# Cross-attention and a mixture of experts: ranks counted in sets of tiles, one-hots beside attention, returns by products of 32 columns, warm-up products

## The reference

```python
def _L0_xattn_ref(q, k, v):
    ...
    qh = q.reshape(b * h, d // h, m)
    kh = k.reshape(b * h, d // h, -1)
    vh = v.reshape(b * h, c // h, -1)
    ...
    qk = jnp.einsum('bdm,bdn->bmn', qh, kh) * scale
    sm = jax.nn.softmax(qk, axis=-1)
    ret = jnp.einsum('bmn,bcn->bcm', sm, vh)
    return ret.reshape(b, c, m)
...
    gate_logits = jnp.einsum('bsd,de->bse', x, gate_kernel)
    top_k_weights, top_k_indices = jax.lax.top_k(gate_logits, TOP_K)
    top_k_weights = jax.nn.softmax(top_k_weights.astype(jnp.float32), axis=-1).astype(x.dtype)
    ...
    out = jnp.einsum('bse,bsem,emd->bsd', combine, inter, wo_kernel)
...
x = x + _L0_xattn_ref(_layernorm(x, axis=-1), ctx_2048, ctx_2048)
x = x + _L0_ffn_ref(_layernorm(x, axis=-1), ...)
```

## Time and profile before

| | us |
|---|---|
| median of 3 runs (lowest, highest) | 517.07 (514.99, 517.77) |
| the profiled execution | 516.18 |
| its span, first to last instruction | 514.4 |
| mean granted TensorE clock | 0.924 of 2.4 GHz |

### The profile page before, as it was taken

One profiled execution on the slowest core, in us unless ns is written; L12 is line 12 of the kernel. 1 busy time (PEld: TensorE's weight loads), 2 busy tenths in 40 slices (PEclk: granted clock), 3 DMA queues, 4 the chain that ended last, 5 costly groups with the idle time before them and its releaser, 6 DMA issues.

```text
span 514.4 us, 10299 instructions
## 1 busy us (share of the span) xinstructions
PE 446.7 (87%) x3238; PEld 236.4 (46%) x3239; DVE 283.1 (55%) x594; ACT 239.4 (47%) x472; POOL 216.0 (42%) x235
## 2 busy tenths in 40 slices
PE   3938998998989999888148999999999999999991
PEld 3412343443444443224124666666666666666650
DVE  7898989888779989357794222222222222222220
ACT  2755988887768889573002222222222222222220
POOL 8574040627180522295411444444444444444422
PEclk9865999998889999799557999999999999999997
DMA  8776578768686824159921222223322232223321
GB/s 245 219 221 174 132 200 222 228 192 257 182 238 165 257 97 130 46 205 393 395 97 36 32 51 41 41 41 51 51 41 41 43 50 50 41 41 44 50 28 22
DMA packets 42331, 65.42 MB, mean 127 GB/s; under 512 B 6361, under 2 KB 32154, under 8 KB 42298
## 3 DMA queue, kind: packets, MB, share of 16 engines
q1 hardware_dynamic: 28570, 38.49, 26.2%
q0 software_dynamic: 11424, 24.39, 20.2%
q10 hardware_dynamic: 2304, 2.10, 1.3%
HBM read 40.18 MB, written 24.45 MB: 126 GB/s over the span
## 4 chain that ended last, share of the span: by engine, by line
PE 68%; DVE 12%; ACT 7%; DMA 3%; POOL 3%; issue 2%; SPq 1%; ACTq 1%; POOLq 0%; DVEq 0%
PE max_ps L1432 26%; PE pv_ps L1323 9%; PE ring_ps L1444 6%; PE pv_ps L1444 6%; DVE mx L910 6%; PE ring_ps L1306 6%; ACT pt L766 5%; PE ring_ps L1405 3%; PE max_ps L1204 3%; PE max_ps L1276 2%; PE ring_ps L1395 2%; PE ring_ps L1225 2%; PE ring_ps L1289 2%; SPq L384 1%; DVE K L1108 1%
## 5 line engine op out<-in xcount | busy, mean ns | idle before, releaser
L910 DVE TENSOR_REDUCE mx<-max_ps 128x4 f32<-128x1024 f32 x128 | 150.1, 1215 | 18.3 <-PE max_ps L1204 18.1
L766 ACT ACTIVATE pt<-ring_ps 128x512 f32<-128x512 f32 x256 | 139.1, 598 | 35.1 <-PE ring_ps L1306 31.7
L1432 PE MATMUL max_ps<-w_sb,pt 128*128 x312 | 142.1, 599 | 0.9 <-ACT pt L831 0.9
L703 POOL DMA_INDIRECT out<-rb,sidx x39 | 62.0, 1591 | 119.9 <-DVE gidx L1143 58.5
L1167 DVE TENSOR_TENSOR pt<-pt,max_ps 128x512 f32<-128x512 f32 x39 | 26.8, 687 | 121.7 <-PE max_ps L1432 62.7
L1432 PEld LDWEIGHTS max_ps<-w_sb,pt 128*128 128x128 f32 x312 | 57.0, 193 | 58.1 <-issue 58.1
L1323 PE MATMUL pv_ps<-pt,w_sb 128*27 128x256 f32 (+2 forms) x1024 | 81.1, 401 | 1.8 <-ACT pvs L776 1.0
L1204 PE MATMUL max_ps<-K,Q 48*128 48x256 bf16 x512 | 53.4, 289 | 11.6 <-DVE mx L910 11.6
L1306 PE MATMUL ring_ps<-Q,K 50*128 50x256 f16 x512 | 53.1, 288 | 11.6 <-ACT pt L766 10.2
L838 ACT ACTIVATE pt<-ring_ps 128x512 f32<-128x512 f32 x39 | 23.3, 597 | 71.9 <-PE ring_ps L1405 71.9
L695 POOL DMA_INDIRECT pt<-xrow,gidx x39 | 38.7, 992 | 30.3 <-DVE gidx L1118 11.1
(11 more groups left out here) (175 smaller groups left out, 437.2 us busy)
## 6 DMA issues: line engine op xcount, KB each, us to landing
w_sb<-in_L_ffn_w_kernel POOLq DMA_DIRECT2D x16, 512.0 KB, 10.1
K<-k_img SPq DMA_DIRECT2D x14, 448.0 KB, 6.1
Q<-q_img SPq DMA_DIRECT2D x14, 448.0 KB, 7.5
k_img<-kpart SPq DMA_DIRECT2D x28, 192.0 KB, 3.8
q_img<-qpart SPq DMA_DIRECT2D x28, 192.0 KB, 3.4
wo_sb<-in_L_ffn_wo_kernel POOLq DMA_DIRECT2D x8, 512.0 KB, 12.6
acc<-pvs SPq DMA_DIRECT2D x6, 512.0 KB, 3.1
q_sb<-in_x SPq DMA_DIRECT2D x16, 128.0 KB, 4.1
```

Of the source, the lines that this page charges most:

```text
L703: g.indirect_dma_start(xacc, bass.IndirectOffsetOnAxis(ap=sidx[sl.par][:, 0:1], axis=0), y_sb[sl.par], None, compute_op=ALU.add).then_inc( ...
L766: a.activation(pt[:, (2 * i + h) % PTN, :, :], bank(key)[:, :, :], ACT.Exp, scale=SCALE).then_inc(ring_read, 1)
L910: v.tensor_reduce(mx[:, t % 2, :, :, p].rearrange("q mt h -> q h mt"), max_ps[n % 2][:, :, :, :], axis=AX.X, op=ALU.max).then_inc(max_read, 1)
L1432: last = nc.tensor.matmul(flat(max_ps[sl.par][:, bank_of]), lhsT=xT[sl.par][:, k * P:(k + 1) * P], rhs=weight(w, e, KC, k), start=(k == 0) ...
```

## The change

- The four returns to token layout are made of four products of 32 columns each, all into `max_ps[0]`, at steps (14,1), (14,4), (15,2) and after the last; each but the first waits for the residual of the one before.
- `turn_rows` of units 5 and 6 and their logits move to (15,1) to (15,4).
- Ranks are counted in three sets of tiles: 0 to 7, 8 to 13, 14 and 15. For each set PE multiplies `cnt` of all its tiles with the triangle and with ones (`rank`; at (15,0), at (15,7) in front of the last `pv`, and behind the last logits). VectorE (`ranks`) sums over tiles and works out the place in the tile at once, since an expert's start is a multiple of 128; `onehots` makes the set's `onehot_s`, now with two operations and two scalars of each partition, so that it carries the token number. `told` for token numbers goes away.
- The last residual stands in front of the last two choices but behind the choice, the count and the ranks of tiles 8 to 13; the one-hots of tiles 8 to 13 stand behind the last normalisation.
- Behind the last rank product: three warm-up products of 512 columns, one and two more behind the table of tokens and the spare rows.
- The sum of `e2` and `spare` (what GpSimd's reciprocal waits for) come behind `onehot_t`; the weights of slots are divided by the token number (`rtok`).

```diff
-    rows_at[T - 1, 3] = ST - 3
-    logits_at[T - 1, 5] = ST - 3
-    rows_at[T - 1, 6] = ST - 2
+    rows_at[T - 1, 1] = ST - 3
+    logits_at[T - 1, 2] = ST - 3
+    rows_at[T - 1, 3] = ST - 2
+    logits_at[T - 1, 4] = ST - 2
+    unperm_at = {(T - 2, 1): 0, (T - 2, 4): 1, (T - 1, 2): 2}
+    rank_sets = (range(T - 8), range(T - 8, T - 2), range(T - 2, T))
+    ranks_at = {(T - 1, 0): 0, (T - 1, 7): 1}
...
+            def ranks(m):
...
+                v.wait_ge(ranks_full, m + 1)
...
+                for j, t in enumerate(tiles):
+                    then(v.tensor_tensor(before_t[:, t + 1] if t + 1 < T else total[:, :], before_t[:, t], of_tile[:, j], ALU.add))
+                v.tensor_tensor(before_t[:, to], before_t[:, to], in_tile, ALU.add).then_inc(ranks_read, 1)
+                v.wait_ge(ranks_read, m + 1)
...
+                then(v.tensor_tensor(prod, A[:, :, to], before_t[:, None, to].broadcast_to([P, TOPK, n, E]), ALU.mult))
+                then(v.tensor_reduce(slot[:, :, to], prod, axis=AX.X, op=ALU.add))
+                then(v.tensor_copy(slot_i[:, 0, :, to], slot[:, :, to]))
+                then(v.tensor_scalar(slot_i[:, 1, :, to], slot_i[:, 0, :, to], P - 1, None, ALU.bitwise_and))
+                then(v.tensor_copy(slot_f[:, 0, :, to], slot_i[:, 1, :, to]))
+                then(v.tensor_tensor(slot[:, :, to], slot[:, :, to], slot_i[:, 1, :, to], ALU.subtract))
+
+            def onehots(m):
+                for k in range(TOPK):
+                    for t in rank_sets[m]:
+                        v.tensor_scalar(onehot_s[:, k, t, :], iota_s[:, :], slot_f[:, 0, k, t:t + 1], token1f[:, t:t + 1],
+                                        ALU.is_equal, ALU.mult).then_inc(told_done, 1)
...
-            choose(ST - 5, range(T - 8))
+            choose(ST - 5, rank_sets[0])
+            count(0)
             norm_last(normed_last[0:2], x2_last[0:2], 0, 1)
-            count(1, range(T - 8))
+            ranks(0)
+            onehots(0)
 
             residual_last(2)
             stats_last(x2_last[2:3], 2)
-            choose(ST - 3, range(T - 8, T - 4))
+            choose(ST - 2, rank_sets[1])
+            count(1)
             norm_last(normed_last[2:3], x2_last[2:3], 2, 2)
-            count(2, range(T - 8, T - 4))
-            choose(ST - 2, unit_tiles[ST - 2])
-            count(3, unit_tiles[ST - 2])
+            ranks(1)
 
             residual_last(3)
             stats_last(x2_last[3:4], 3)
             choose(ST - 1, unit_tiles[ST - 1])
             norm_last(normed_last[3:4], x2_last[3:4], 3, 3)
-            count(4, unit_tiles[ST - 1])
+            onehots(1)
             choose(ST, unit_tiles[ST])
-            count(5, unit_tiles[ST])
...
+            count(2)
+            ranks(2)
...
-                pe.wait_ge(pv_read, T - 4 + i + 1)
-                for which, to in ((1, 1), (0, 0)):
-                    for f, a, b in ((0, 0, 96), (1, 96, P)):
-                        last = nc.tensor.matmul(max_ps[i % 2][a:b, to, 0, :], lhsT=unperm[:, which, a:b], rhs=pvs[:, f, i % 2, :],
...
+                for which in (1, 0):
+                    for q in range(4):
+                        at = slice(32 * q, 32 * q + 32)
+                        last = nc.tensor.matmul(max_ps[0][at, which, 0, :], lhsT=unperm[:, which, at], rhs=pvs[:, q // 3, i % 2, :],
...
+            def rank(m):
...
+                pe.wait_ge(count_done, m + 1)
+                for b, with_ in ((0, tri), (P, ones)):
...
+            def keep_warm(n):
+
+                for _ in range(n):
+                    nc.tensor.matmul(flat(max_ps[1][:, 1]), lhsT=ident[:, :], rhs=flat(xn), start=True, stop=True)
...
+                if (t, p) in ranks_at:
+                    rank(ranks_at[t, p])
             pv(T - 1, 3, 0)
             pv(T - 1, 3, 1)
             unpermute(3)
...
+            rank(2)
+            pe.wait_ge(ranks_read, 2)
+            keep_warm(3)
+
+            pe.wait_ge(told_done, TOPK * T)
+            for k in range(TOPK):
+                pe.wait_ge(rows_picked, k + 1)
...
```

More of the change, by code:

```diff
@@ L77, in xattn_ffn_kernel @@
             slots["logits", logits_at[t, p]] = len(slots)
-    for n in range(ST - 2, UNITS):
-        if n > ST - 2:
-            slots["rows", n] = len(slots)
+    for n in range(ST - 1, UNITS):
+        slots["rows", n] = len(slots)
         slots["logits", n] = len(slots)
@@ L818, in _ @@
             evac_pv(T - 1)
-            for m in range(ST - 2, UNITS):
-                if m > ST - 2:
-                    evac_rows(m)
+            for m in range(ST - 1, UNITS):
+                evac_rows(m)
                 evac_logits(m)
-            a.wait_ge(gap_done, 5)
+            a.wait_ge(gap_done, 4)
             a.activation(e2[:, :], gap[:, :], ACT.Exp).then_inc(e2_done, 1)
@@ L988, in then, with count @@
                 v.wait_ge(chain, links[0])
-            def count(m, tiles):
-                v.wait_ge(top_done, m)
+            def count(m):
+                tiles = rank_sets[m]
                 a, n = tiles[0], len(tiles)
@@ L995, in count @@
                                      iota_e[:, None, None, :].broadcast_to([P, TOPK, n, E]), ALU.is_equal))
[L996 to L1002, removed]
+                v.tensor_tensor(cnt[:, a:a + n], A[:, 0, a:a + n], A[:, 1, a:a + n], ALU.add).then_inc(count_done, 1)
@@ L1037, in _ @@
             then(v.memset(before_t[:, 0], 0.0))
-            for k in range(TOPK):
-                then(v.tensor_copy(pay[:, 0, k, :], token1[:, :]))
+            then(v.tensor_copy(token1f[:, :], token1[:, :]))
             lead_e = E // 2
@@ L1062, in _ @@
             norm_last(normed_last[3:4], x2_last[3:4], 3, 3)
-            count(4, unit_tiles[ST - 1])
+            onehots(1)
             choose(ST, unit_tiles[ST])
-            count(5, unit_tiles[ST])
[L1067 to L1075, removed]
+            count(2)
+            ranks(2)
+            then(v.tensor_scalar(tiles_i[:, 0], total[:, :], float(P - 1), None, ALU.add))
             then(v.tensor_scalar(tiles_i[:, 1], tiles_i[:, 0], P - 1, None, ALU.bitwise_and))
@@ L1084, in _ @@
                 shift *= 2
[L1086 to L1090, removed]
@@ L1091, in _ @@
-            then(v.tensor_scalar(slot_i[:, 1], slot_i[:, 0], P - 1, None, ALU.bitwise_and))
-            then(v.tensor_tensor(slot_f[:, 1], slot[:, :, :], slot_i[:, 1], ALU.subtract))
+            base = ends[end][:, lead_e - 1:lead_e + E - 1]
+            then(v.tensor_tensor(A[:, :, :, :], A[:, :, :, :], base[:, None, None, :].broadcast_to([P, TOPK, T, E]), ALU.mult))
+            then(v.tensor_reduce(slot_f[:, 1], A[:, :, :, :], axis=AX.X, op=ALU.add))
+            then(v.tensor_tensor(slot_f[:, 1], slot_f[:, 1], slot[:, :, :], ALU.add))
@@ new lines, in _ @@
+                if k == 0:
+                    onehots(2)
+            v.wait_ge(e2_done, 1)
+            v.tensor_scalar(norm[:, :], e2[:, :], 1.0, None, ALU.add).then_inc(norm_in, 1)
+            then(v.scalar_tensor_tensor(spare[:, :, :], cnt[:, :, :], 0.0,
+                                        token1[:, :, None].broadcast_to([P, T, E]), op0=ALU.is_equal, op1=ALU.mult))
+            v.tensor_reduce(spare_own[:, :], spare.rearrange("p t e -> p e t"), axis=AX.X, op=ALU.max).then_inc(spare_done, 1)
@@ L1144, in next_gather @@
                                 ALU.add).then_inc(gidx_done, 1)
-            v.wait_ge(slots_done, 1)
+            then(v.tensor_scalar(rtok[:, :], tok[:, :], 1.0, None, ALU.max))
+            then(v.reciprocal(rtok[:, :], rtok[:, :]))
             then(v.tensor_tensor(spare_of[:, :], spare_of[:, :], spare_own[:, :], ALU.add))
```

125 lines of the change are left out of this document (68 added, 57 removed).

## The result

| | before | after |
|---|---|---|
| median (lowest, highest) of 20 runs each | 517.33 (514.99, 521.52) | 513.99 (506.77, 515.59) |
| the profiled execution | 516.18 | 510.25 |
| its span | 514.4 | 508.5 |
| mean granted clock | 0.924 | 0.925 |

The account below looks back on a forecast made before the run. VectorE, nearly alone, was taken to bound the stretch before the PE-bound expert loop. Savings of 0.7 (last reciprocal), 3.25 (to the first tile's turn) and 0.5 (clock) made 4.4 us: 512.7 from the median, range 508.8 to 518.0.

Parts of the forecast that it names:

- the sum of 4.4: Whole kernel: 0.7 at the last reciprocal, 3.25 from there to the first gathered tile's turn, 0.5 by clock: 4.4 us saved.
- its own signs of being wrong: No stall at rank(1); one-hots not 0.165; 16 return products over 2 us; first gather bound by anything else; slower loop.
- Weights and first normalisation: During attention: first weight issue at 217.8 instead of 222.51, VectorE's normalisation at 227.4 instead of 232.11, 4.7 us gained there.
- A return: Return to token layout by 16 products of 32 columns: about 1.3 us at full clock, bounds 1.3 and 4.7.
- First stall: PE at rank(0), reached at about 219.4, waits 2.2 us for VectorE's count until 221.6; absorbed later.
- One-hots, the term that was mis-sized: VectorE's one-hots at 0.165 us each: 16 before rank(1) take 2.65, 12 take 2.0 hidden, the last 4 0.66.
- small terms dearer: Rival: one-hots at 0.25 us each, or ranks 0.3 more a step; 515.0 us, reads as no change; chance 0.21.
- The stall at `rank(1)`: PE, done at about 233.9, waits 6 us before attention's last output products for VectorE's count at 240.0; last reciprocal 244.3.
- What the reordering promises ... is eaten by the stall: At the last reciprocal: 240.2 if only the return were awaited, but PE's stall leaves 244.3, a gain of 0.7.
- both arms: Two paths to the last reciprocal: PE's return, ready at 244.3 (242.8 at full clock), and VectorE's ranks, done at 243.4.
- R to the turn: From the last reciprocal's start to PE's turn of the first gathered tile: 22.65 us instead of 25.9, 3.25 less.
- Clock: First expert's products after the warm-ups: 0.5 us saved, bounds 0 and 1.8, the clock more likely falling again, only later.

Follow-up runs that it names:

- `rank(0)` late: The changed kernel with the first rank product at (15,2) instead of (15,0); single run 512.84 us, beside a median of 516.95 for the kernel before.
- Reciprocal early: The changed kernel with the sum that GpSimd's reciprocal needs put in front of the ranks of the last two tiles; ratio 0.9862 to the kernel before.

## Why the prediction came out as it did

The range and the sign were right, the time 1.3 us off the median; against the traces the sum of 4.4 stands beside 5.9 us of span. Counted from G to the end of the first products it is 5.5 (65.7 before, 60.2 after), since G came 0.3 us earlier in the second trace. Of its own signs of being wrong one came true: one-hots were not at 0.165. Term by term:

- **Weights and first normalisation.** Forecast 217.8 and 227.4; measured 217.85 and 227.45. That the issues would stand in front of the rstd was right.
- **A return.** 1.3 forecast, 1.07 measured, at full clock. The Trainium skill, "TensorEngine Tiling (Array Packing)", section "Theoretical Speedup", allows up to 4x. Against the prediction's 4.7 us for 16 products one after another, an estimate from the wide ones, 1.07 is 4.4x; against the old return of 2.37, which had half as many products, it is 2.2x.
- **First stall.** 2.2 forecast, 2.30 measured, and free, as `rank(0)` late shows. The fall to half clock behind it was not foreseen; it cost nothing either.
- **One-hots, the term that was mis-sized.** 0.165 was carried over from a form with one pointer; the new one runs at 0.229. That is 1.0 us in the first set, on the longer arm to `rank(1)`, which came at 240.69 where 240.0 was forecast. It is the case "small terms dearer" of the rivals, at 0.23 rather than 0.25. The 12 took 2.75 instead of 2.0, which all but hid in the wait for the last logits (PE had made them at 252.17, VectorE took them at 252.41, with no idle time in front), and the last 4 0.89 instead of 0.66.
- **The stall at `rank(1)`.** 6 forecast, 4.57 measured, PE having reached it at 236.1 and not at 233.9: the third return and the logits had run at half clock. Its end is VectorE's, so R came at 244.79 instead of 244.3: gain 0.17, not 0.7, and none (-0.1) when both are counted from G. The terms named for R, 240.0 + 0.3 + 2.0 + 0.7 + 1.1, add up to 244.1; 0.2 of the 244.3 has no term. The prediction had both arms, with VectorE's ranks done at 243.4 (measured 243.98) and the return at 244.3. Its step "What the reordering promises ... is eaten by the stall" still blames the wrong one: the two end 0.8 us apart, and VectorE's would have held R without any stall. Without the stall R would be 0.8 earlier; without the wait of VectorE for the rstd, 5.5 earlier.
- **R to the turn.** 22.65 forecast, 22.06 measured. To the last count 8.7 (8.5), product and back 0.39 (0.45), ranks 1.85 (1.9), ends and tiles 2.35 (2.3), one-hots 2.34 (2.3), sum and reciprocal 3.17 (3.2). The one step that was off is the last: from the reciprocal's end to the turn 3.26 instead of 4.0, because a gather's preparation of 0.7 us runs beside the reciprocal when it waits in the queue behind it. Before, the queue was empty and the preparation followed the index. Reciprocal early shows both sides.
- **Clock.** 0.5 forecast within bounds of 0 and 1.8; measured 1.55 on the products and 0.25 on the turn. The forecast took 3.8 us to lie between the last warm-up and the products, with a turn in it, and a fall of the clock in that time. It was 1.87: the last warm-ups ran partly at half clock (four in 2.99 us, where full clock takes 1.98) and ended at R + 21.5 instead of R + 20.3, and the turn came 0.6 earlier than forecast.
- **Loop.** From the start of the first products to the end 242.0 before and 240.35 after; but for the 1.55 the loop is the same.

So the errors were -0.5 us at R, +0.6 behind it and +1.3 at the clock, with 0.1 left of the 1.5. That the first two cancel is luck; the main miss is the 1.3 at the clock. That the median nonetheless fell by only 3.3 is the other runs of the kernel after: the profiled one lay 3.7 below their median, that of before 1.2 below its own.

## What to carry to other kernels

When two arms join, look at each one's waits, not only at the idle engine: the 4.6 us in front of `rank(1)` were worth 0.8, while a wait of 6.4 us on the busy engine, with independent work queued behind it, was worth 5.5. A form that takes one more scalar of each partition should be timed before it is used: 0.06 us each was 1.0 us for 16 of them on the path. Warm-up products have to be sized to end just before their data lands: with R at W + 21.4, longer ones delayed the turn and shorter ones lost the clock, and the end of the first products stayed within 0.2 us.

## What the runs showed of the hardware

- **A second pointer scalar** costs 0.06 us on 128x128 in 16 bit (0.228 against 0.169), a second operation with an immediate nothing.
- **Warm-up products do not by themselves make the next products fast.** With a pause of 0.64 us or less between them and the turn, the first products took 3.69 to 3.70 in all six traces. With 1.0, 1.45 and 1.6 us they took 5.39 in three. A fourth (the run with 32 more one-hots: last warm-up over at 270.1, turn at 271.72) had 1.6 us and 3.70, so the pause alone does not decide it. What does stays open. The Trainium skill, "TensorE: Matmul & The Clock Gate", Part 1, says that activity releases the throttle; the traces agree in that the clock rises during the warm-ups (the second group's pair took 1.56 us here, 1.13 where the clock was full), and that without them it stayed at 0.50 until the products.
- **Faster warm-up products leave a longer pause.** Where the last four ran at full clock (1.98 us) and the gather waited for the reciprocal as in the kernel after, the pause was 1.45 to 1.6 us (three traces); where they took 2.92 to 2.99 us it was 0.53 to 0.64 (three traces).
- **GpSimd prepares an indirect gather beside the operation in front of it.** It starts 0.19 us behind a reciprocal of 2.92 in the kernel after, but 0.94 behind the index where nothing runs in front of it (reciprocal early, and the kernel before).
